# The causal mask of the maximum pass: one full-height product per head in place of two half-height ones

## The reference, cut to what matters

```python
scores = jnp.einsum('bhqd,bhkd->bhqk', q, k) / SCALE
causal_mask = jnp.arange(seq)[None, :] > jnp.arange(seq)[:, None]
scores = jnp.where(causal_mask, jnp.float32(-1000000000000.0), scores)
probs = jax.nn.softmax(scores, axis=-1)
attn = jnp.einsum('bhqk,bhkd->bhqd', probs, v)
```

## Time and profile before

| | |
|---|---|
| time, median of 3 runs | 1750.98 us (1750.64, 1750.98, 1761.45) |
| span of the profiled execution | 1759.6 us, mean granted PE clock 0.958 |
| PE, matmuls | 1587.2 us busy (90%), 12430 of them |
| PEld, weight loads | 1099.6 us (62%) |
| DVE | 1401.9 us (80%) |
| ACT | 955.8 us (54%) |
| POOL | 915.0 us (52%) |

### The profile page before, as it was taken

How to read it: one execution, slowest core, us unless ns; L and a number is a source line. 1 busy time by engine, 2 the same in 40 slices (tenths; PEclk the granted TensorE clock), 3 DMA queues, 4 the chain that set the end, 5 groups by cost and what they waited for, 6 DMA issues and landing times.

```text
span 1759.6 us, 34071 instructions
## 1 busy us (share of the span) xinstructions
PE 1587.2 (90%) x12430; PEld 1099.6 (62%) x12430; DVE 1401.9 (80%) x2672; ACT 955.8 (54%) x1562; POOL 915.0 (52%) x973
## 2 busy tenths in 40 slices
PE   4899999889899999999989999999999999989950
PEld 2774555555566555445445877788888877778740
DVE  5779877677787878778796998888898899989942
ACT  2741556566666666555743556565555665535620
POOL 5207877651665475678776146622221365654256
PEclk9879999999999999999999999999999999999985
DMA  7963689989999776667448567665666577668413
GB/s 229 303 158 132 186 223 261 273 267 249 283 292 259 214 193 163 153 187 195 119 125 264 165 199 229 195 211 173 192 209 201 185 224 232 189 196 252 132 58 91
DMA packets 277959, 354.69 MB, mean 202 GB/s; under 512 B 32272, under 2 KB 204304, under 8 KB 272416
## 3 DMA queue, kind: packets, MB, share of 16 engines
q1 hardware_dynamic: 237600, 287.92, 57.1%
q0 software_dynamic: 17056, 33.66, 6.9%
q10 hardware_dynamic: 23136, 30.94, 5.1%
HBM read 197.48 MB, written 122.68 MB: 182 GB/s over the span
## 4 chain that ended last, share of the span: by engine, by line
PE 43%; DVE 23%; POOL 9%; issue 9%; DMA 7%; SPq 5%; ACT 4%; ACTq 0%; DVEq 0%; POOLq 0%
PE Y L1124 7%; PE R L867 5%; PE R L900 5%; PE R L869 5%; PE R L868 5%; POOL gat L1408 4%; DVE row_max L1997 3%; POOL xs_dram L1432 3%; DVE state L2098 3%; PE R L883 3%; PE Y L1018 2%; DMA q_rows<-kq 2%; DVE hid L2146 2%; DMA fw<-wf 2%; DVE dw L2092 1%
## 5 line engine op out<-in xcount | busy, mean ns | idle before, releaser
L1432 POOL DMA_INDIRECT xs_dram<-sc_in,pos x256 | 265.1, 1036 | 150.8 <-issue 58.7
L1408 POOL DMA_INDIRECT gat<-ys_dram,pos x256 | 262.6, 1026 | 125.3 <-issue 62.3
L1997 DVE TENSOR_REDUCE row_max<-R 128x6 f32<-128x768 f32 x256 | 238.9, 951 | 63.5 <-PE R L982 58.4
L900 PE MATMUL R<-ident_b 128*128 128x512 bf16 x936 | 255.8, 394 | 32.3 <-DVE K L1850 26.3
L1452 POOL TENSOR_TENSOR o_acc<-o_acc,read 128x512 f32<-128x512 f32 x112 | 146.1, 1304 | 263.8 <-DVE read L2108 262.7
L1124 PEld LDWEIGHTS Y<-fd,hid 128*128 128x128 f32 (+1 forms) x1824 | 232.3, 192 | 53.7 <-DVE hid L2146 25.9
L1604 ACT ACTIVATE probs<-R 128x768 f32<-128x768 f32 x256 | 203.8, 809 | 105.4 <-PE R L1006 99.2
L1124 PE MATMUL Y<-fd,hid 128*128 128x128 f32 (+1 forms) x1824 | 249.9, 280 | 11.3 <-DVE hid L2146 10.7
L1443 POOL TENSOR_SCALAR_AFFINE_SELECT probs<-probs 128x512 f32<-128x512 f32 x256 | 169.8, 664 | 158.1 <-ACT probs L1604 155.1
L867 PE MATMUL R<-fhl,fw 128*128 128x512 f32 x418 | 182.2, 436 | 1.3 <-DVE fhl L2136 1.3
L1723 ACT ACTIVATE sil<-R 128x512 f32<-128x512 f32 x190 | 112.9, 596 | 127.9 <-PE R L869 83.3
(11 more groups left out here) (270 smaller groups left out, 3399.6 us busy)
## 6 DMA issues: line engine op xcount, KB each, us to landing
fw<-wf SPq DMA_DIRECT2D x38, 1408.0 KB, 7.8
q_rows<-kq SPq DMA_DIRECT2D x128, 256.0 KB, 5.1
fx<-xs_dram SPq DMA_DIRECT2D x86, 256.0 KB, 3.4
xs_dram<-gat SPq DMA_DIRECT2D x24, 512.0 KB, 4.9
qk_dram<-qk_parts SPq DMA_DIRECT2D x32, 384.0 KB
Q<-qk_dram SPq DMA_DIRECT2D x64, 192.0 KB
K<-qk_dram SPq DMA_DIRECT2D x64, 192.0 KB
fw<-wf SPq DMA_DIRECT2D x96, 128.0 KB
```

The costliest lines, as they stand in the source:

```text
L900: pe.matmul(psum["R"][:, b * C:(b + 1) * C], ident_b[:, :], ident_b[:, :].unsqueeze(1).to_broadcast([P, TILES, P]), start=True, stop=True)
L1408: pool.indirect_dma_start(gat[:, i % 2, 2 * t + a, :], None, ys_dram[l][g], bass.IndirectOffsetOnAxis(ap=pos[l][g][a][:, col:col + 1], axi ...
L1432: pool.indirect_dma_start(xs_dram[g], bass.IndirectOffsetOnAxis(ap=pos[l][g][a][:, col:col + 1], axis=0), sc_in[:, n % 2, t * P:(t + 1) * ...
L1997: dve.tensor_reduce(row_max[:, b, h2, :, :], pair[:, :].rearrange("p (g c t) -> p g c t", g=2, t=P)[:, :, 0:3, :], AX.X, ALU.max).then_inc ...
```

## The change

The mask of a head becomes one product of 128 rows: `ident_b` (the identity in bf16, the same that the fillers use) times `causal`, read twice, over 2 x 128 columns. B1 issues two such products in place of four of 64 rows. The copies `ident_h` and `causal_h` are still made. Beside it, ACT's stage C1b waits for the turn of the chunk before, in the planner's table and in the code.

```diff
-            stage(t + 16, "C1b", n, after=[("C1", n, 0, "POOL")], DVE=0.1, ACT=2.1)
+            stage(t + 16, "C1b", n, after=[("C1", n, 0, "POOL")], DVE=0.1, ACT=(2.1, since(n, 1, ("C2", 0, "PE"))))
...
-                    for j in range(2):
-                        for g, bank in enumerate(banks):
-                            rows = slice(64 * g, 64 * g + 64)
-                            ins = pe.matmul(bank[:, 0:3 * P].rearrange("p (c t) -> p c t", t=P)[:, 0:3:2, 64 * j:],
-                                            ident_h[rows, j, :], causal_h[rows, j, :, 64 * j:], start=False, stop=j == 1,
-                                            skip_group_check=True)
+                    for bank in banks:
+                        ins = pe.matmul(bank[:, 0:3 * P].rearrange("p (c t) -> p c t", t=P)[:, 0:3:2, :], ident_b[:, :],
+                                        causal[:, :].unsqueeze(1).to_broadcast([P, 2, P]), start=False, stop=True,
+                                        skip_group_check=True)
                     ins.then_inc(pair.full, 1)
...
                 if kind == "C1b":
                     if n >= 1:
                         wait(*x1n_saved(n - 1))
+                        wait(*bank_of["xT1", n - 1].filled())
```

## The result

The changed kernel is slower by 0.35%: ratio 1.0035, 95% interval 1.0022 to 1.0049, medians 1759.5 against 1751.4 us of 21 runs each. Two more comparisons gave 1.0016 (0.9997 to 1.0035) and 1.0029 (1.0012 to 1.0046). The three weighted together are 1.0029 (1.0020 to 1.0038), which is **+5 us (3.4 to 6.6)**. The forecast was +16: right in sign and inside its range, but three times too large, and under what I had called the lower end, 11 us.

What follows compares the result with a forecast made beforehand. No single engine was taken to bound the kernel, PE setting the pace in somewhat under half the time. 11.0 us on the chain plus 5 of the remaining 17.6 gave +16, 1767 us; range 1752 to 1785.

Steps and rivals of the forecast that it cites:

- What bounds the kernel: From 120 to 850 us no single engine carries the chain of waits; PE has 323 of 730 us, DVE 194.
- The prices: Per stage B1: +0.045 us before whole-array work, +0.24 before split rows, +0.15 before line 1018; 28.6 us PE time in all.
- A rule weighed: Changing tiling mode drains TensorE: each new switch would cost 0.16 us, not 0.09 to 0.105; judged less than a drain.
- With all else as it was they are paid in full: the lower end: The chain crosses mask line 982 in 109 of 256 stages B1; the added 11.0 us there reach the end.
- A bit under a third of the 17.6, 5 us: Of 17.6 us added PE time off the chain, 5 us are paid, as slipping stages often make PE the path.
- Hidden: Another route is nearly as long as PE's, or later queueing shortens: only 0 to +8 us remain; chance 0.11.
- PE is the path nearly everywhere: Slack is used up at once and nearly all 28.6 us is paid: +22 to +29 us; chance 0.27.
- PE pays by the product: Fixed price per mask product, two taking 0.085 us: 0.085 saved at each of 109 places, -9 us; chance 0.05.
- The products are dearer than half a filler: New mask products take 0.13 to 0.24 us each: +5 us at 0.13, beyond 1790 us at 0.24; chance 0.04.
- What would show it: Signs in the changed profile: 0.20 us from line 977, 0.21 to a filler, attention's last maximum some 16 us later.

Runs made afterwards that it cites:

- both halves of the change: Against the kernel before: the change only in 153 stages B1 followed by whole-array work, +4 us (1 to 7); only in the other 103, +8 us (4 to 11).
- switch_only: Kernel before plus a 128-row, 2-column product between line 977 and the half-height mask products: +29 us (24 to 35), repeated on another chip +22 (17 to 27).
- no_mask_switch: Kernel before without mask products, with a 128-row, 2-column product between lines 974 and 977: +16 us (12 to 19).

## Why the prediction was right or wrong

**What bounds the kernel**: right that no engine does. PE's share of the chain, 0.44, came close to the 0.38 that the fit gives for a us of PE time at an unchanged clock; the runs whose clock moved by 0.003 or less lie between 0.34 and 0.54, the change itself (0.16) apart.

**The prices**: right. 0.205 - 0.109 = 0.096 for the way in (0.09 forecast), 0.32 to split rows and to line 1016 (0.32), 0.23 to a filler (0.215); the last result is there 0.096 + 0.39 = 0.49 us after the first mask product would have started (0.47); the sum was 32 and not 28.6 us. The dearer switch that was weighed under "A rule weighed", 0.16 us, did not come either: 0.11 us after a product of 2 columns started, the next one starts, while its own row is 0.18 long. C1b's edit was priced at nothing, and no run tests that by itself.

**"With all else as it was they are paid in full: the lower end"**: this step failed. The sum put 11.0 us on the path as a floor, and 5 (3.4 to 6.6) came out. All else isn't as it was when PE's work changes: over the runs the granted clock went from 0.914 to 0.973, and in this change up by 0.002 to 0.004. The rows of before had the sign in plain sight: a clock of 0.95 between 300 and 500 us, in a kernel that issues 936 products whose results nobody reads. 12 us (7 to 16), what both halves of the change cost together at an unchanged clock, is about what the 11.0 of the chain meant. Off it come, by the fit's 1.1 to 1.4 us for each 0.001, an estimated 3 to 4 us that the clock gives back; the rest of the way to 5, some 3 to 4 us, lies within the intervals of the halves, and its cause stays open. So the clock is shown to move the time of this kernel; that it makes up the whole miss isn't.

**"A bit under a third of the 17.6, 5 us"**: by the whole change wrong too. I expected PE to become the path more often and to cost more for it. It did become the path more often (424 us of the chain, some 400 in the second profile), and no more came out for it; the two halves cost 0.33 to 0.4 a us, no more than the chain's share. Their sum's interval just reaches the 16 of the forecast, so at an unchanged clock this term isn't refuted by them alone.

**Hidden (0.11)** is the rival that came true in size, 0 to +8, but hardly for the reason it gave, another route of nearly the same length: both halves cost near the chain's share, and the clock rose. Whether another route has a part in the open 3 to 4 us, no run shows. **PE is the path nearly everywhere** fell even at +88 us of PE time, where +29 came out. **PE pays by the product** fell by 0.23 us for two products where 0.085 was its bound. **The products are dearer than half a filler** fell too: 0.23 / 2 = 0.115 us each, its case began at 0.13. **What would show it** named an end of the attention that has not moved as a sign of being wrong, and so it was, 850.6 us against 850.8; but that sign was weaker than I took it for, since the profile of before is of an execution with a low clock (0.958) and a span 8.6 us over the median, and the second profile of the changed kernel has 853.4.

## What to carry to other kernels

Before costing an edit on TensorE, read the granted clock beside it: where it is under full, work that you add or remove can move the clock as well, and the sum over durations of one execution is only half of the answer. The chain's share of an engine was here a fair price for a us of its time while the clock held. One profile is one execution: before two are compared, their spans and clocks should be held against the medians of their kernels. A lower bound from a chain holds only as long as every duration on it stays what it was.

## What the runs showed of the hardware

- Going from products on split rows to one over the whole array costs 0.096 us, and the way back 0.10 to 0.11, for products of 2 as of 256 columns: one of 2 columns between the two costs 0.21 us in all (`switch_only`).
- Busy time in the rows and the granted clock need not move together: in `no_mask_switch` the first rose (679 to 686 us) and the second fell (0.97 to 0.95). Products of 2 columns amid switches went with a lower clock (0.957 and 0.963 against 0.960 and 0.966), full ones in less PE time with a higher one (0.971 and 0.968 against 0.965 and 0.966).
- Within one kernel the clock varies too: over 29 executions of before, from 0.957 to 0.970, and the time falls by 1.1 us for each 0.001 (correlation -0.78). Which of the two leads there is not shown. The profile that the prediction was made from had 0.958, near the low end; 0.007 under the mean of these 29 is 8 us by that slope, and its span lay 8.6 us over the median.
